# Residual scales folded into matrices, one cast moved to POOL, and six of eight second MLP products as three rounded passes

## What is computed

```python
q, k, v = (t @ Wqkv + bqkv) split           # q = relu(q) * scale, k = relu(k)
ctx = einsum('bhnd,bhne->bhde', k, v)
out = einsum('bhnd,bhde->bhne', q, ctx)
img = depthwise_conv_3x3(out) + dw_b
out = img @ Wproj + bproj
t = bn1(t + out) + alpha1 * (t + out)        # a scale s1 and a shift per channel
ff = gelu(t @ Wfc1 + bfc1, approximate=False) @ Wfc2 + bfc2      # 128 -> 1024 -> 128
t = bn2(t + ff) + alpha2 * (t + ff)          # a scale s2 and a shift per channel
x = x + t
```

## Time and profile before

| | |
|---|---|
| median of 3 runs | 2737.96 us (2734.21 to 2738.51) |
| profiled execution | 2738.23 us |
| its span, first to last instruction | 2736.4 us |
| busy share of the span | PE 92%, DVE 80%, ACT 78%, POOL 50% |
| mean granted TensorE clock | 0.986 of full |
| third stage, 1366 to 2690 us | PE busy 1324.0 of 1324 us, ACT 1177.7, DVE 1057.8, POOL 667.9 |

### The profile page before, as it was taken

How to read it: one execution, slowest core, us unless ns; L and a number is a source line. 1 busy time by engine, 2 the same in 40 slices (tenths; PEclk the granted TensorE clock), 3 DMA queues, 4 the chain that set the end, 5 groups by cost and what they waited for, 6 DMA issues and landing times.

```text
span 2736.4 us, 106560 instructions
## 1 busy us (share of the span) xinstructions
PE 2521.7 (92%) x43050; PEld 2019.7 (74%) x43050; DVE 2186.2 (80%) x4859; ACT 2134.5 (78%) x3977; POOL 1380.4 (50%) x1378
## 2 busy tenths in 40 slices
PE   2888888888888998899799999999999999999999
PEld 1666666666666666698688888888888888888887
DVE  4888888888888888667778887888878888788885
ACT  2777677767776777566688988889888898888987
POOL 1555455545554555466345545545455454544544
PEclk9999999999999999899899999999999999999999
DMA  4222122212221111244201110111101111000000
GB/s 140 70 73 74 57 89 67 74 57 89 74 67 51 48 54 54 81 137 123 80 31 41 37 41 31 41 41 37 41 31 41 40 38 41 31 28 18 19 21 21
DMA packets 55794, 152.17 MB, mean 56 GB/s; under 512 B 6608, under 2 KB 20944, under 8 KB 55632
## 3 DMA queue, kind: packets, MB, share of 16 engines
q1 hardware_dynamic: 55632, 149.93, 17.2%
HBM read 98.52 MB, written 51.38 MB: 55 GB/s over the span
## 4 chain that ended last, share of the span: by engine, by line
PE 72%; DVE 18%; issue 4%; ACT 2%; POOL 2%; DMA 1%; DVEq 0%; SPq 0%; POOLq 0%; ACTq 0%
PE bank L1282 14%; PE bank L1283 14%; PE bank L1284 14%; PE bank L1535 12%; DVE mx L967 7%; PE bank L1437 6%; PE bank L1336 4%; DVE vx L960 3%; PE bank L1299 2%; ACT prob L672 2%; DVE gst L1012 1%; PE bank L1347 1%; DVE xc L953 1%; PE bank L1450 1%; POOL lnrs L514 1%
## 5 line engine op out<-in xcount | busy, mean ns | idle before, releaser
L608 POOL TENSOR_TENSOR hl<-hf,hh 128x448 fp32r<-128x448 f32 x448 | 516.8, 1154 | 661.3 <-ACT hh L818 661.3
L1172 DVE SCALAR_TENSOR_TENSOR bank<-oring,dw,bank 128x448 f32<-128x448 f32 x896 | 614.5, 686 | 20.1
L1535 PE MATMUL bank<-hw,w 128*128 128x448 f32 x896 | 390.7, 537 | 0.0
L815 ACT ACTIVATE hf<-bank,fc1b 128x448 f32<-128x448 f32 x448 | 282.1, 630 | 135.1 <-PE bank L1284 135.1
L1282 PE MATMUL bank<-t1h,w_hi 128*128 128x448 f32 x896 | 369.4, 412 | 5.4 <-DVE t1l L1189 5.4
L1283 PE MATMUL bank<-t1h,w_lo 128*128 128x448 f32 x896 | 330.3, 369 | 0.0
L1284 PE MATMUL bank<-t1l,w_hi 128*128 128x448 f32 x896 | 330.0, 368 | 0.0
L818 ACT ACTIVATE hh<-hf 128x448 fp32r<-128x448 f32 x448 | 259.6, 579 | 14.2
L809 ACT ACTIVATE hw<-bank,fc1b 128x448 f32<-128x448 f32 x448 | 265.8, 617 | 0.4 <-PE bank L1284 0.4
L967 DVE TENSOR_REDUCE mx<-bank 128x8 bf16<-128x512 f32 x448 | 248.2, 616 | 10.2 <-PE bank L1316 7.4
L520 POOL TENSOR_TENSOR xn_lo<-xn,xn_hi 128x512 fp32r<-128x512 f32 x112 | 128.7, 1149 | 251.1 <-ACT xn_hi L649 251.1
(11 more groups left out here) (164 smaller groups left out, 6586.0 us busy)
## 6 DMA issues: line engine op xcount, KB each, us to landing
ximg<-x SPq DMA_DIRECT2D x112, 448.0 KB, 3.4
ximg<-x_in SPq DMA_DIRECT2D x56, 448.0 KB, 3.5
x<-ximg SPq DMA_DIRECT2D x56, 448.0 KB, 2.5
y_out<-yb SPq DMA_DIRECT2D x112, 224.0 KB, 2.0
xs<-x_in SPq DMA_DIRECT2D x42, 448.0 KB, 3.4
wm<-wm_in SPq DMA_DIRECT2D x1, 512.0 KB, 4.1
w1f<-w_in SPq DMA_DIRECT2D x1, 512.0 KB, 5.1
w<-w_in SPq DMA_DIRECT2D x1, 512.0 KB, 6.5
```

The lines of the kernel that those rows point to most:

```text
L608: g.tensor_tensor(hl[:, k, :], hf[:, k % 2, :], hh[:, k, :].bitcast(F32), ALU.subtract).then_inc(hl_ready, 1)
L815: a.activation(hf[:, k % 2, :], bank[j % FC1_BANKS][:, 0:BLOCK], ACT.Gelu, bias=fc1b[:, j:j + 1]).then_inc(hf_ready, 1)
L1172: m = d.scalar_tensor_tensor(acc, src, dw[:, k:k + 1], acc, ALU.mult, ALU.add)
L1535: m = mm(out, w2[:, j, :], hw[:, WHOLE_J.index(j), :], start=first, stop=last)
```

## The change

The scale s1 is multiplied into the columns of Wproj, and s2 into those of Wfc2, once, before they are rounded. The shift of the first residual goes through Wfc1 into a bias of the hidden layer for each image (`fc1i`), and the shift of the second is one constant an image and channel (`ycon`). With that `mix` becomes x times a scale plus the bank, in one DVE instruction from `ximg`, and ACT loses `scaled_x` and the `wb` of `t1_high`. The sum `xw` = s2 t1 + x, which POOL made from `wb`, becomes a DVE instruction `skip` behind `t1_low`. The rounded query `qh`, which ACT made from the bank, is now a copy of `qf` on POOL (`q_round`), issued behind the second `hl` of a block. `SPLIT_J` becomes 0, 1, 2, 3, 5, 6, so that two more of the second products are split. The one-time work is: two diagonal matrices and one fp32 product that broadcasts s1 and s2, a DVE multiply of all of w2 and one of Wproj in the first stage, the rounding of two more slices of w2, sixteen four-column products and one DVE add for `fc1i` before the third stage.

```diff
-SPLIT_J = (0, 2, 3, 5)
+SPLIT_J = (0, 1, 2, 3, 5, 6)
@@ POOL
-            def residual_d(B, b, bb):
-                pool.wait_ge(wb_ready, B + 1)
-                g.tensor_tensor(xw[:, bb, :], wb[:, bb, :], ximg[:, bass.ds(b * BLOCK, BLOCK)],
-                                ALU.add).then_inc(xw_ready, 1)
+            def q_round(B, bb):
+                pool.wait_ge(qf_ready, B + 1)
+                hold(pool)
+                g.tensor_copy(qh[:, bb, :], qf[:]).then_inc(qh_ready, 1)
@@ POOL step_d
                     g.tensor_tensor(hl[:, k, :], hf[:, k % 2, :], hh[:, k, :].bitcast(F32),
                                     ALU.subtract).then_inc(hl_ready, 1)
-                if near(1):
-                    residual_d(B + 1, at(1)[1], (u + 1) % 2)
+                    if k == 1 and near(4):
+                        q_round(B + 4, u % 2)
@@ ACT
-            def q_high(B, image, bb, prev=True, n=4):
+            def q_relu(B, image, prev=True, n=4):
-                a.activation(qf[:], bank[n][:, 0:BLOCK], ACT.Relu, bias=qb[:, image:image + 1])
-                a.activation(qh[:, bb, :], bank[n][:, 0:BLOCK], ACT.Relu, bias=qb[:, image:image + 1])\
-                    .then_inc(qh_ready, 1)
+                a.activation(qf[:], bank[n][:, 0:BLOCK], ACT.Relu, bias=qb[:, image:image + 1]).then_inc(qf_ready, 1)
-            def scaled_x(i, b, bb):
-                a.activation(ub[:, bb, :], ximg[:, bass.ds(b * BLOCK, BLOCK)], ACT.Identity,
-                             bias=gpar[:, i, 1:2], scale=gpar[:, i, 0:1]).then_inc(u_ready, 1)
                 a.activation(t1h[:, bb, :], t1[:, bb, :], ACT.Copy).then_inc(t1h_ready, 1)
-                a.activation(wb[:, bb, :], t1[:, bb, :], ACT.Identity, bias=par_("K2"),
-                             scale=par_("s2")).then_inc(wb_ready, 1)
-                             bias=fc1b[:, j:j + 1]).then_inc(hf_ready, 1)
+                             bias=fc1i[:, j, image:image + 1]).then_inc(hf_ready, 1)
@@ DVE, once
+            def late_scale():
+                dve.wait_ge(late_loaded, 32)
+                dve.wait_ge(scale_read, 1)
+                d.tensor_tensor(w2[:], w2[:], sbc[:, 1:2, :].to_broadcast([P, NF, P]), ALU.mult)
+                d.tensor_tensor(wmat("wproj"), wmat("wproj"), sbc[:, 0, :], ALU.mult).then_inc(late_scaled, 1)
@@ DVE
-            def mix(B, bb):
-                dve.wait_ge(u_ready, B + 1)
+            def mix(B, image, b, bb):
                 dve.wait_ge(proj_mm, B + 1)
-                d.scalar_tensor_tensor(t1[:, bb, :], bank[4][:, 0:BLOCK], par_("s1"), ub[:, bb, :],
-                                       ALU.mult, ALU.add).then_inc(t1_ready, 1)
+                hold(dve)
+                d.scalar_tensor_tensor(t1[:, bb, :], ximg[:, bass.ds(b * BLOCK, BLOCK)], gpar[:, image, 0:1],
+                                       bank[4][:, 0:BLOCK], ALU.mult, ALU.add).then_inc(t1_ready, 1)
+            def skip(B, b, bb):
+                d.scalar_tensor_tensor(xw[:, bb, :], t1[:, bb, :], par_("s2"), ximg[:, bass.ds(b * BLOCK, BLOCK)],
+                                       ALU.mult, ALU.add).then_inc(xw_ready, 1)
@@ DVE finish
-                d.scalar_tensor_tensor(yb[:, bb, :], bank[6 + bb][:, 0:BLOCK], par_("s2"), xw[:, bb, :],
-                                       ALU.mult, ALU.add).then_inc(y_ready, 1)
+                d.scalar_tensor_tensor(yb[:, bb, :], bank[6 + bb][:, 0:BLOCK], ycon[:, image:image + 1],
+                                       xw[:, bb, :], ALU.add, ALU.add).then_inc(y_ready, 1)
@@ DVE step_d
                 if near(1):
                     t1_low(B + 1, (u + 1) % 2)
+                    skip(B + 1, at(1)[1], (u + 1) % 2)
                 taps_ahead(7, NTAP)
@@ PE step_d
-                            pe.wait_ge(qh_ready, B + 5)
+                            pe.wait_ge(qf_ready, B + 5)
                         project(B + 1)
@@ PE, once
+            def shifted_bias():
+                pe.wait_ge(gpar_ready, 1)
+                pe.wait_ge(qf_ready, 1)
+                for j in range(NF):
+                    for k in range(2):
+                        m = mm(bank[0][:, NIMG * j:NIMG * (j + 1)], w1s[k][:, P * j:P * j + P].bitcast(F32),
+                               gpar[:, :, 1], start=(k == 0), stop=(k == 1))
+                m.then_inc(fc1i_mm, 1)
```

More of the change, by code:

```diff
@@ L118, in build @@
         gpar = sb("gpar", [P, NIMG, 2])
+        ycon = sb("ycon", [P, NIMG])
+        fc1i = sb("fc1i", [P, NF, NIMG])
+        sbc = sb("sbc", [P, 2, P])
         def v(name, n=1):
@@ L282, in build @@
         t1l_ready = sem("t1l_ready")
-        wb_ready = sem("wb_ready")
         xw_ready = sem("xw_ready")
+        qf_ready = sem("qf_ready")
+        fc1i_mm = sem("fc1i_mm")
+        fc1i_ready = sem("fc1i_ready")
+        scale_ready = sem("scale_ready")
+        scale_mm = sem("scale_mm")
+        scale_read = sem("scale_read")
+        late_scaled = sem("late_scaled")
         h_mm = sem("h_mm")
@@ L609, in step_d @@
                                     ALU.subtract).then_inc(hl_ready, 1)
-                if near(1):
-                    residual_d(B + 1, at(1)[1], (u + 1) % 2)
-            residual_d(0, 0, 0)
+                    if k == 1 and near(4):
+                        q_round(B + 4, u % 2)
+            for k in range(4):
+                q_round(k, k % 2)
             block_loop(pool, step_d)
@@ L620, in _ @@
             act.wait_ge(consts_loaded, 16 * NCONST)
-            a.activation(pws[0][:], wm[:, 0:2, :], ACT.Copy)
-            a.activation(pjs[0][:], wmat("wproj"), ACT.Copy).then_inc(weights_hi, 1)
+            a.activation(pws[0][:], wm[:, 0:2, :], ACT.Copy).then_inc(weights_hi, 1)
             act.wait_ge(par_ready, 1)
             def late_high():
-                act.wait_ge(late_loaded, 32)
+                act.wait_ge(late_scaled, 1)
                 a.activation(w1s[0][:], w1f[:], ACT.Copy)
+                a.activation(pjs[0][:], wmat("wproj"), ACT.Copy)
                 for k, j in enumerate(SPLIT_J):
@@ L853, in _ @@
             t1_high(0, 0)
+            act.wait_ge(fc1i_ready, 1)
             block_loop(act, step_d)
@@ L1040, in step @@
                 norms = at_norms(i, s) and gg == 0
+                if norms and i == 0:
+                    late_scale()
                 if norms:
@@ L1083, in _ @@
             m.then_inc(gst_ready, 1)
+            scales_read()
             dve.wait_ge(par_ready, 1)
@@ L1140, in _ @@
                     dve.wait_ge(bias_ready, NIMG)
+                    d.tensor_scalar(gpar[:, :, 0], gc[:, 1, :, 0], par_("s1"), None, ALU.mult)
+                    d.tensor_scalar(gpar[:, :, 1], gc[:, 1, :, 1], par_("s1"), par_("K1"), ALU.mult, ALU.add)\
+                        .then_inc(gpar_ready, 1)
+                    dve.wait_ge(gpar_ready, 1)
+                    d.tensor_scalar(ycon[:], gpar[:, :, 1], par_("s2"), par_("K2"), ALU.mult, ALU.add)\
+                        .then_inc(gpar_ready, 1)
             def tb_low(B, b, bb):
@@ L1215, in step_d @@
                 if near(1):
-                    mix(B + 1, (u + 1) % 2)
+                    mix(B + 1, *at(1), (u + 1) % 2)
                 if near(5):
@@ L1237, in _ @@
             q_low(3, 1)
+            dve.wait_ge(fc1i_mm, 1)
+            d.tensor_tensor(fc1i[:], bank[0][:, 0:NF * NIMG].rearrange("p (j i) -> p j i", i=NIMG),
+                            fc1b[:].unsqueeze(2).to_broadcast([P, NF, NIMG]), ALU.add).then_inc(fc1i_ready, 1)
             dw_low(0)
             taps(1, 1, 0, 4, 0)
-            mix(0, 0)
+            mix(0, 0, 0, 0)
             taps(1, 1, 4, NTAP, 0)
             t1_low(0, 0)
+            skip(0, 0, 0)
             block_loop(dve, step_d)
-            finish(NB - 1, NIMG * STRIPS - 1, 1, True)
+            finish(NB - 1, NIMG - 1, NIMG * STRIPS - 1, 1, True)
         @block.tensor
@@ L1253, in _ @@
             mm(bank[7][:, 0:1], wmat("wproj"), v("dwb"), start=True, stop=True).then_inc(cb_mm, 1)
+            pe.wait_ge(scale_ready, 1)
+            mm(bank[6][:, 0:2 * P], obc[:, 2, :], obc[:, 0:2, :].rearrange("p a b -> p (a b)"), start=True, stop=True)\
+                .then_inc(scale_mm, 1)
             pe.wait_ge(weights_lo, 1)
@@ L1562, in _ @@
             for k in range(4):
+                if k == 2:
+                    shifted_bias()
                 if k >= 2:
@@ L1568, in _ @@
             project(0)
+            pe.wait_ge(fc1i_ready, 1)
             block_loop(pe, step_d)
```

38 lines of the change are left out of this document (18 added, 20 removed).

## The result

The changed kernel takes **2881.28 us** (median of 4 runs, 2878.1 to 2884.74), the kernel before, on the same chip, 2736.09 us (4 runs, 2734.02 to 2738.51). The ratio is **1.0527** (95% interval 1.0512 to 1.0542), +145 us. It is slower, as forecast, and inside the range, but 71 us above the forecast. The case that came is B, which was the second likeliest; the range took in A, B and C.

A forecast was written before the change was run, and what follows sets the result against it. PE's queue was taken to bound the third stage, at 12.23 us a block. The profiled 2738.2 us plus 2 for one-time work plus 70 for the blocks with ql going first gave 2810 us, range 2760 to 2905.

The forecast's parts named there:

- case B: Rival: hl 2 takes the DVE/POOL path before ql, which is held; 13.66 us a block, 2894 us; chance 0.33.
- case A: Forecast case: ql takes the DVE/POOL path before hl 2; 12.6 to 13.15 us a block, 2810 us; chance 0.42.
- Case C: Rival: DVE and POOL do not hold each other; 12.53 us a block, 2772 us; chance 0.10.
- What bounds the kernel, and PE's saving: Third stage: PE's queue sets the time; two wholes becoming six passes save 0.27 us, leaving 11.96 a block.
- Case D: Rival: PE's queue stays the bound if hl 5 ends by 9.74; 11.96 us a block, 2710 us; chance 0.07.
- ACT's chain: ACT's steps in a block: from hf 0, hf 2 starts at 2.82 us and hh 6 at 8.38.
- The sixth hl: hl 5 on POOL ends at 10.19, PE wants it at 9.80 for fc2 6; 12.53 us a block, +0.30.
- The shared path: A DVE instruction with two SBUF inputs and a POOL instruction shut each other out; who comes first goes first.
- The cast: The query's rounding to fp32r on POOL, 448 columns: taken as 0.56 us.
- Who goes first: ql on DVE or hl 2 on POOL after the cast: left open, POOL leading by some 0.03 us.
- One-time work: Added scale multiplies, roundings and products ahead of the third stage: taken +2 us, bounds -1 and +5.
- The marks named beforehand: Signs: PE waits 0.5 us or more before fc2 6, PE share under 0.97, DVE waits over a microsecond, ql or hl 2 long.

The follow-up runs named there:

- order: Changed kernel with t1h on ACT behind j = 6, tap 3 on DVE ahead of ql, skip behind the last tap; 2714.02 us, ratio 0.9925.
- t1h_later: Changed kernel with t1h on ACT behind j = 6 instead of j = 5, nothing else; 2854.74 us, ratio 1.0416.
- all_psum: Changed kernel with ql, tbl, t1l and skip each reading one input from PSUM instead of SBUF (output changed); 2768.83 us, ratio 1.0101.
- gap_wide_b: Changed kernel with an unused 256-column POOL memset between the query's cast and hl 2; 2784.09 us, ratio 1.0145.
- gap: Changed kernel with an unused 8-column POOL memset between the query's cast and hl 2; 2876.99 us, ratio 1.0522.
- before_six: Kernel before with six splits (SPLIT_J = 0, 1, 2, 3, 5, 6) and nothing else of the change; 2894.95 us, ratio 1.0551.
- dve_order: Changed kernel with only DVE's order changed: tap 3 ahead of ql, skip behind the last tap; 2790.56 us, ratio 1.0174.

## Why the prediction was partly wrong

The direction was right and the time inside the range, but the range held three cases, and the one taken as the forecast did not come.

**What bounds the kernel, and PE's saving: right.** The queue of 11.96 us a block was worked out from passes of 0.2055 and wholes of 0.75. In "order" a block is 11.97. That the two agree within 0.01 is in part luck: the passes were 0.0025 shorter than taken, 0.1 us a block, and PE loses as much before fc2 6. Case D's condition (hl 5 at most 9.74 after hf 0, that is 0.45 us less ahead of it on ACT) was right as one condition: moving t1h's 0.47 behind it gave 9.66 and 2714 us, against the 2710 of case D. It was not enough by itself: t1h_later makes the same move on ACT and takes 2855 us, because DVE's chain is then last.

**ACT's chain: right.** Worked out 2.82 from hf 0 to hf 2 and 8.38 to hh 6; in "order", 2.81 and 7.86, with t1h's 0.47 no longer ahead: 8.33.

**The sixth hl: right, and a little too large.** Case C's block was 12.53 and its time 34 us above before; all_psum gave blocks of 12.44 (ql at 2000.86 and 2013.30), that is +0.21 instead of +0.30, and +1.01%, 28 us.

**The shared path: right**, and with it the direction. Holds appear at ql, tbl, t1l and skip or at an hl, up to about the length of the other side's instruction.

**The cast: right**, 0.559 us in the mean, against 0.56 taken.

**Who goes first: the step that failed.** The prediction worked out that ql would start 0.03 behind hl 2, and that is what it did (2014.13 against 2014.10). It then gave case A, ql first, 0.42 and case B 0.33, on the ground that DVE, "level with POOL", had won in the earlier trace rows. But in that pair DVE led by 0.01 (2012.49 to 2012.50), so it spoke for the sentence a few lines above it, who comes first goes first, and by that sentence a lead of POOL's, however small, means case B. I read a pair that showed the rule as if it showed a preference for DVE. What the runs show in its place: with hl 2 0.02 to 0.04 ahead, ql took 1.6 in 106 blocks of the changed kernel, and 1.0 us of hold stands at the head of DVE's chain. With B as the likeliest the forecast would have been 2894, 13 us off instead of 71. gap_wide_b shows that the rest of case A was sound: with ql made first the block is 12.56, at its lower end, by the path that case A gave for it (hl 5 between t1l and skip, then DVE's last taps).

**Case B's size.** 13.66 worked out, 13.49 measured, 0.17 too much. POOL starts the next instruction some 0.06 before the recorded end of the one before (cast at 2013.54, hl 1 until 2013.60), so ql ended and t started 0.07 to 0.08 earlier than laid out (t at 6.98 after hf 0 instead of 7.06). t1l took 0.85, not 0.93, and the last steps the rest. Over the stage it is 1.25 a block against 1.43: -19 us.

**One-time work: neither borne out nor refuted.** Taken +2; in this profile the third stage starts 11.3 us later. But in the profiles of the twelve runs that have the new one-time work its first fc1 pass stands anywhere from 1360.35 (gap) to 1375.87 (the changed kernel), 1369.8 in the mean. Before it is 1364.53, and in before_six, which has none of the scales' work, 1374.10. The first two stages vary by some 15 us from one profile to the next, so no run here can tell +2 from nothing. What the spread comes from is open.

**The marks named beforehand** all came as case B had them: PE waits for hl before fc2 6 (0.72), PE's share 0.94 (under 0.97), DVE waits 1.2 us for the cast, and ql, not hl 2, is 1.6 long.

## What to carry to other kernels

Before work moves between DVE and POOL, list for each POOL instruction that reads SBUF which DVE instruction with two SBUF inputs can start within its duration, and ask who leads; here a lead of 0.03 us decided over a whole instruction, and a DVE instruction that waited for a POOL result while POOL had its next instruction ready lost each time. What such a hold costs depends on what is queued behind it: put work that doesn't need the result (a tap) ahead of the wait, put what is needed late (the skip) behind what is needed early, and put nothing ahead of the last product's inputs that can come after them. Where a change saves time on the bounding engine and comes out slower, try its order before dropping it: three moved steps turned +5.3% into -0.75% here.

## What the runs showed of the hardware

- Who starts first decides, down to the smallest leads in the record. In the five runs with ql 0.01 to 0.05 behind hl 2 (the changed kernel, gap, dve_order, order, t1h_later) ql took 1.59 to 1.63 in all 532 such blocks; in the seven blocks where ql led, by 0.01 to 0.03, ql took 0.62 or 0.63 and hl 2 took 1.60 to 1.64. An hl 0.04 behind xw took 1.63 instead of 1.15.
- The held side ends before the holder's end and its own length would add up to: ql, 0.62 long by itself, ended 0.49 after hl 2 did (2015.74 against 2015.25).
- A DVE instruction that waits for POOL's result starts 0.03 to 0.04 after the recorded end of it (2014.10 to 2014.13, 2012.37 to 2012.41), while POOL's own next instruction, if it is ready, starts at that end or up to 0.06 before it (2013.54 against 2013.60). So POOL led whenever hl 2 was ready. In the odd block of the changed kernel its hh ended only at 1785.75; the cast ended at 1785.76, ql started at 1785.80 and hl 2 at 1785.83.
- An 8-column memset between two POOL instructions moved the second by nothing (2012.38 against a cast that ended at 2012.37), one of 256 columns by 0.2 us (2020.75 against 2020.55).
- With one input in PSUM the same DVE subtraction takes 0.63 beside an hl that started 0.04 earlier; with both in SBUF, 1.6.
- At a granted clock of 1.00 the passes of a split product stood 0.205 us apart in the profiles of the kernel before, before_six and gap, and 0.202 to 0.203 in those of the other runs. Why is not shown; it is 0.1 us a block.
